# Two key pairs of node tiles to each step of the edge loop, and the twelve steps that this moves everything behind it

## What is computed

```python
xn = layernorm(x)
# 1. graph attention over the edges
Wh = xn @ W_w + W_b
e  = leaky_relu((Wh @ a_w[:256])[dst] + (Wh @ a_w[256:])[src] + a_b[0], 0.2)
att = segment_softmax(e, src)
g  = relu(segment_sum(att[:, None] * Wh[dst], src))
# 2. linear attention over all nodes, 8 heads
q, k = elu(xn @ Wq.T) + 1, elu(xn @ Wk.T) + 1;  v = xn @ Wv.T
m  = (q (k^T v) / max(q . sum(k), 1e-6)) @ Wproj.T + bproj
x  = x + g + m
# 3. mixture of 8 experts, two of them for each node
t  = layernorm(x);  combine = top-2 of softmax(t @ router_w.T), renormalised
out = x + t + sum_e combine[:, e] * (gelu(t @ w1[e] + b1[e]) @ w2[e] + b2[e])
```

## Time and profile before

| | before |
|---|---|
| median of 3 runs | 2332.44 us |
| lowest, highest | 2324.99, 2332.51 us |
| profiled execution, its own time | 2342.57 us |
| its span | 2340.8 us |
| PE, DVE, ACT, POOL busy, share of the span | 76%, 72%, 40%, 42% |
| granted TensorE clock, mean | 0.862 |

### The profile page before, as it was taken

One profiled execution on the slowest core, in us unless ns is written; L12 is line 12 of the kernel. 1 busy time (PEld: TensorE's weight loads), 2 busy tenths in 40 slices (PEclk: granted clock), 3 DMA queues, 4 the chain that ended last, 5 costly groups with the idle time before them and its releaser, 6 DMA issues.

```text
span 2340.8 us, 40197 instructions
## 1 busy us (share of the span) xinstructions
PE 1768.7 (76%) x13588; PEld 1284.2 (55%) x13588; DVE 1674.4 (72%) x4215; ACT 934.8 (40%) x2258; POOL 984.9 (42%) x996
## 2 busy tenths in 40 slices
PE   4788886651666676578888757887788787899998
PEld 2557573441455564466666535555555555666666
DVE  5888898652665667667676668888888878865665
ACT  6222221121222222222222236656656566666564
POOL 3000002425655566655555666666666566100000
PEclk7788797785878887788988869989999999999999
DMA  5011111113545543333333333333333348300000
GB/s 164 6 55 49 48 62 30 45 60 90 140 129 137 137 126 106 93 101 102 100 99 96 83 91 83 85 90 94 81 91 84 91 81 88 35 10 10 10 19 12
DMA packets 121715, 182.20 MB, mean 78 GB/s; under 512 B 21614, under 2 KB 92158, under 8 KB 121470
## 3 DMA queue, kind: packets, MB, share of 16 engines
q0 software_dynamic: 45568, 120.06, 21.8%
q1 hardware_dynamic: 75904, 59.25, 8.1%
HBM read 152.43 MB, written 26.63 MB: 76 GB/s over the span
## 4 chain that ended last, share of the span: by engine, by line
DVE 37%; PE 31%; issue 14%; another core or an unknown queue 9%; ACT 4%; DVEq 2%; POOL 1%; DMA 1%; ACTq 0%; SPq 0%; POOLq 0%
PE bank L1197 6%; PE bank L1213 6%; DVE big L1458 4%; DVE mloc L1541 3%; DVE big L1463 3%; DVE work L1536 3%; DVE work L1519 2%; PE bank L928 2%; DVE big L1460 2%; DVE big L1465 2%; DVE scr L1563 2%; DVE work L1737 2%; PE bank L903 1%; PE bank L1083 1%
## 5 line engine op out<-in xcount | busy, mean ns | idle before, releaser
L631 POOL DMA_INDIRECT work<-table,tiles x904 | 906.8, 1003 | 574.0 <-PE bank L1065 312.4
L1213 PE MATMUL bank<-big 128*128 128x256 f16 x2352 | 314.2, 277 | 0.3 <-issue 0.3
L1063 PE MATMUL bank<-work,scr 128*128 128x257 f16 x904 | 277.7, 307 | 36.5 <-issue 22.1
L1064 PE MATMUL bank<-work,scr 128*128 128x256 f16 x904 | 279.4, 309 | 14.8 <-issue 14.8
L1065 PE MATMUL bank<-work,scr 128*128 128x257 f16 x904 | 279.4, 309 | 12.5 <-issue 12.5
L1197 PE MATMUL bank<-scr,big 128*128 128x512 f16 (+1 forms) x1248 | 280.3, 374 | 4.1 <-ACT big L838 2.9
L1031 PE MATMUL bank<-identh,work 128*128 128x128 f16 x904 | 85.3, 250 | 247.1 <-DVE work L1536 209.7
L1213 PEld LDWEIGHTS bank<-big 128*128 128x128 f16 x2352 | 233.8, 99 | 35.7 <-issue 0.5
L1563 DVE SCALAR_TENSOR_TENSOR scr<-scr,gg,bank 128x257 f32<-128x257 f32 x452 | 217.9, 482 | 38.3 <-issue 15.2
L954 PE MATMUL bank<-big 128*128 128x208 f16 x1568 | 172.6, 264 | 72.9 <-DVE big L1465 62.2
L1031 PEld LDWEIGHTS bank<-identh,work 128*128 128x128 f16 x904 | 64.8, 112 | 278.8 <-DVE work L1536 229.0
(11 more groups left out here) (337 smaller groups left out, 3383.3 us busy)
## 6 DMA issues: line engine op xcount, KB each, us to landing
work<-table,tiles POOLq DMA_INDIRECT x904
scr<-normed_cols SPq DMA_DIRECT2D x98, 128.0 KB
table<-big SPq DMA_DIRECT2D x49, 129.0 KB, 2.2
normed_rows<-scr SPq DMA_DIRECT2D x49, 128.5 KB, 2.8
big<-normed_rows SPq DMA_DIRECT2D x49, 128.5 KB
normed_cols<-big SPq DMA_DIRECT2D x49, 128.0 KB, 2.7
xs<-in_x_dram SPq DMA_DIRECT2D x4, 1536.0 KB, 14.6
out_dram<-work SPq DMA_DIRECT2D x48, 128.0 KB
```

Source lines behind the costliest of these rows:

```text
L631: pool.indirect_dma_start(G[:, r, j, :], None, table, bass.IndirectOffsetOnAxis(ap=col[:, t:t + 1], axis=0)).then_inc(rows_in[r // GS], 16)
L1063: pe.matmul(of[:, 0:D + 1], hi, Gh[:, r, j, 0:D + 1], start=(j == 0), stop=False)
L1064: pe.matmul(of[:, 0:D], hi, Gh[:, r, j, D + 2:2 * D + 2], start=False, stop=False)
L1213: mm = pe.matmul(of, hTp[ph][:, k % 2, f, (j + c) * P:(j + c + 1) * P], w2p[pw][:, e, f, :], start=False, stop=(f == 1 and m == 2))
```

## The change

`K_AT` gives each step from -1 to 11 two pairs of node tiles (the last step one), so that the keys end at step 11 and not 23. `CTX_AT`, `A_AT` and `F_AT` are counted from there and all come 12 steps earlier (13, 18 to 42, 51 on); the last expert step is 12 steps earlier too. The experts' weights are placed behind the keys, in steps 14, 16, ... 28, and `b2` at step 30. The two pairs of a step use two banks (7 and 1), two `kk` and two pairs of `ev` and `rv`; PE does both `keys` of a step first and then both `key_sums`. SP asks for columns one step ahead of the rows. In the node table SP sends the rows of tile i + 2, the columns of i + 1 and the table's row of i - 1 in one round. ACT's `norms` is cut into halves, two tiles at the end of one step and two at the end of the next.

```diff
-        kk = q_[0].rearrange("p a b -> p (a b)").rearrange("p (j c) -> p j c", j=2)
+        kk = [v.rearrange("p a b -> p (a b)").rearrange("p (j c) -> p j c", j=2) for v in q_]
...
+        evs, rvs = (ev, qd), (rv, mm_)
...
-        K_AT = {p - 1: p for p in range(PW)}
+        K_AT = {s: range(2 * s + 2, min(2 * s + 4, PW)) for s in range(-1, -(-PW // 2) - 1)}
         CTX_AT = max(K_AT) + 2
         A_FROM = CTX_AT + 5
         A_AT = {A_FROM + p: p for p in range(PW)}
-        P_AT = {1 + 2 * n: n for n in range(2 * PIECES)}
-        assert max(P_AT) < CTX_AT
+        P_AT = {CTX_AT + 1 + 2 * n: n for n in range(2 * PIECES)}
+        B2_AT = max(P_AT) + 2
+        K_BANK = (7, 1)
...
# SP, the node table
-            for i in range(W):
-                rows, r, q = slice(i * P, (i + 1) * P), i % XR, i % TR
-                sp.wait_ge(n_xn, i + 1)
-                sp.dma_start(normed_rows[rows, :], xn[r]).then_inc(rows_out[r], 16)
-                sp.wait_ge(n_xnT, i + 1)
-                sp.dma_start(normed_cols[rows, :], xnT[r].rearrange("p h n -> p (h n)")).then_inc(cols_out[r], 16)
-                sp.wait_ge(n_fd, i + 1)
-                sp.wait_ge(n_lo, i + 1)
-                sp.dma_start(table[rows, :], tab[q]).then_inc(table_out[q], 16)
+            for i in range(-2, W + 1):
+                if i + 2 < W:
+                    sp.wait_ge(n_xn, i + 3)
+                    sp.dma_start(normed_rows[of_tile(i + 2), :], xn[(i + 2) % XR]).then_inc(rows_out[(i + 2) % XR], 16)
+                if 0 <= i + 1 < W:
+                    sp.wait_ge(n_xnT, i + 2)
+                    sp.dma_start(normed_cols[of_tile(i + 1), :], xnT[(i + 1) % XR].rearrange("p h n -> p (h n)")
+                                 ).then_inc(cols_out[(i + 1) % XR], 16)
+                if i > 0:
+                    sp.wait_ge(n_fd, i)
+                    sp.wait_ge(n_lo, i)
+                    sp.dma_start(table[of_tile(i - 1), :], tab[(i - 1) % TR]).then_inc(table_out[(i - 1) % TR], 16)
...
# SP, the edge loop
             for s in range(-1, NS):
-                if s in K_AT:
-                    p = K_AT[s]
-                    if p > 1:
-                        sp.wait_ge(k_ps, p - 1)
+                if s == -1:
+                    for p in K_AT[s]:
+                        turned_rows(p, p)
+                for p in K_AT.get(s + 1, ()):
+                    sp.wait_ge(k_ps, p - 1)
                     turned_rows(p, p)
+                for p in K_AT.get(s, ()):
                     if p > 1:
                         sp.wait_ge(k_sum, p - 1)
                     for j in range(of_pair[p]):
...
# ACT
             def keys_raw(p):
                 n = of_pair[p] * D
                 act.wait_ge(k_ps, p + 1)
-                if p:
-                    act.wait_ge(k_kk, p)
+                if p > 1:
+                    act.wait_ge(k_kk, p - 1)
...
-                for j in range(of_batch[b]):
+                first, n = halves(b)[h]
+                for j in range(first, first + n):
...
                 if s + 3 in FIRST:
-                    norms(FIRST[s + 3])
+                    norms(FIRST[s + 3], 0)
+                if s + 2 in FIRST and of_batch[FIRST[s + 2]] > 2:
+                    norms(FIRST[s + 2], 1)
...
# PE
-                if s - 1 in K_AT:
-                    key_sums(K_AT[s - 1])
-                if s in K_AT:
-                    keys(K_AT[s])
+                for p in K_AT.get(s, ()):
+                    keys(p)
+                for p in K_AT.get(s - 1, ()):
+                    key_sums(p)
...
# DVE
-                if s - 1 in K_AT:
-                    keys_one(K_AT[s - 1])
+                for p in K_AT.get(s - 1, ()):
+                    keys_one(p)
...
-                if s == CTX_AT + 1:
+                if s == B2_AT + 1:
                     dve.wait_ge(loaded["b2"], 16 * 2)
```

43 lines of the change are left out of this document (23 added, 20 removed).

## The result

The changed kernel takes 2269.28 us (median of four, 2266.97 to 2273.09) beside 2331.55 us of the kernel before: a ratio of 0.9747, 95% interval 0.973 to 0.9765. The forecast was 2303.6 us, the range 2273 to 2333. The sign is right, the gain is 62 us where 29 were forecast, and it lies outside the range. The profiled execution took 2273.09 us with a span of 2271.3.

A forecast was written before the change was run, and what follows sets the result against it. The prediction took the chain through the whole edge loop into the experts' matmuls as the bound, with PE ending each key step. Its parts summed to -28.8 us from the median 2332.44 us: 2303.6 us, range 2273 to 2333.

The forecast's parts named there:

- Part 2: Key steps: twelve get a second pair, 16 more float32 matmul records ahead of the spreading, 4.4 us each: +52.8 us.
- Part 1: Edge loop: twelve key steps go and twelve joint steps (edges and experts together) come: +8.6 us.
- part 4: Tail behind the last edges: it loses twelve expert steps of 5.97 us: -71.6 us.
- part 3: Experts' weights leave the key steps, -18.1 us, and land in two context and six query steps, +12.0 us.
- part 5: Norms cut into halves: -1.5 us in nine batches among edges, -0.5 us in four in the tail: -15.5 us.
- part 6: The split of `b2` goes from a context step to a query step: +3 us, between 0 and 6.
- part 7: Node table: SP's new order frees ACT's 104 us wait, but DVE sets the pace: 0, at most -5 us.
- Part 8: SP's loads of columns and rows, four tiles of each a step, cause no wait: taken as 0.
- the second pair comes cheap: Rival, doubled key steps: clock rises from 0.82 to 0.96, 2287 us, or half the pair finds slack, 2277 us; chance 0.23.
- The rule that the forecast cites: Dense matmuls keep PE at full rate; doubled key steps would run at the joint steps' clock: 2287 us.
- The rival of the late release: Key steps: a second pair repeats ACT's delayed release, costing 7.7 us, not 4.4: 2343 us, or slower; chance 0.09.

The follow-up runs named there:

- one pair per step: The change with one pair of node tiles per step again, 25 key steps, all else kept: 2341.15 us in one group, 2323.41 us in another beside the change.
- the version with the loads ahead: The change, weights still behind the keys, with each load of weights issued one step ahead: 2132.44 us, ratio 0.9864, on a quicker chip.
- second profile of the change: The changed kernel itself, unaltered, run again in a later group: 2269.83 us, ratio 0.9746.
- the change with the norms mixed: The change with norms halved only among edges and whole behind the last edges: 2132.84 us, ratio 0.9855, on a quicker chip.
- with filler: The change with one pair of node tiles per step and 32 unread f16 transposes ahead of the turn in the key steps: 2325.44 us, ratio 0.9981.

## Why the prediction was wrong

Its parts against what the runs show (slower chips, the kernel before at 2330 us):

- **Part 2, the second pair, is the step that failed**: +52.8 us forecast, twelve times 4.4. Measured 0.8 us a step (12.76 against 11.96), some 10 us. The forecast's lower end was 0, and its reason was the right one: "the step with one pair is no longer than the contexts' step without". It was set aside with "the first pair has used up the slack". It had not: PE is idle 3.29 us in a step with one pair and 2.05 in one with two. The 48 us of DVE's waiting for PE was read as the price of any further work there. But that wait grew by far less than the work: (48.0 + 16.0) / 25 = 2.6 us a step before, and in the change 50.7 + 2.9 us in 13 steps, 4.1 us. What the runs show in its place, on one chip: the second pair lengthens PE's part of the step by 2.3 us, not by its full 3.4 to 3.8, since the clock goes from 0.85 to 0.96; and the release of the spreading, which came 1.75 us late with one pair, comes 0.23 us late with two. The forecast had read both as PE's work. In the kernel before, more float32 work costs nearly its full length (1.4 to 1.8 us for eight products); in the changed one it costs 0.7. The order itself is worth 0.2 to 0.9 us of a step. Why the release comes on time in the doubled steps stays open.
- **Part 1 and part 4**: twelve steps moved, +8.6 and -71.6 us. Behind the last reduction the change saves 325.3 - 254.9 = 70.4 us against one pair per step, to 1.2 us as forecast.
- **Parts 3, 5, 6 and 7**, forecast -18.1 + 12.0 - 15.5 + 3 + 0 = -18.6 us. One pair per step against the kernel before is these parts together, with the order and the second bank: -6.8 us in one group, +7.9 in another. The norms are the term that was mis-sized: -15.5 forecast, 0 to -4 measured, since the four batches in the tail lose 4.4 us and weren't given a loss. From the profile of the kernel before to that of one pair per step the key steps lose 22.6 us and the queries' gain 18.2, where part 3 has -18.1 and +12.0; the order and the banks lie in these numbers too. Alone, on a quicker chip, moving the weights cost 6 us.
- **Part 8**, loads: no wait, as forecast. What the forecast didn't see is that SP's new wait delays whatever is behind it. It did no harm only because the weights had been moved: with them back in the key steps the time is 49 us longer.

So the sum was wrong by 43 us at the pair and by 12 to 27 us the other way in the rest, and the two partly cancelled: that the total missed by 34 us and not by more is luck.

Three smaller readings of the forecast don't hold. The 1.8 us for which DVE is held before L1632 (part 3) are 26.3 / 23 = 1.1 us by its row. The ends of parts 3, 5 and 6, added up, lie 20.5 us below and 33.5 us above the forecast, where its own range has 13.6 and 13.4. And the ends of parts 5 and 7 are 5.5 and 5 us off, where the floor of the whole range counts 4 for both.

Of the rivals, "the second pair comes cheap" is what happened, and with more than either of its reasons gives. The clock rose as it said, to 0.95, and PE's other work shrank by about the 1.3 us that it counts; the half that it didn't see is the late release that went away, 1.5 us a step. Its other reason, slack in the step with one pair, was right in kind: the slack was this release. The rule that the forecast cites (the Trainium skill, "TensorE: Matmul & The Clock Gate", "Loop structure matters more than you think") is borne out by the granted clock, 0.95 with two pairs and 0.83 to 0.85 with one; the time worked out by it, 2287 us, is still 18 too long. The rival of the late release, at 7.7 us a pair, had the direction wrong: with a second pair the delay did not double, it went.

## What to carry to other kernels

When work is added to an engine that others wait for, the wait says that the engine matters, not that further work costs its full length. Set the engine's idle time per step and the length of the nearest step without such work beside it, read how long after the engine's last record the waiting one starts, and price the addition in the kernel in which it will stand. Before moving a wait on an in-order queue, list what stands behind it: here a load that nobody had touched would have cost most of what the change gave (48 of 62 us). And work packed into fewer steps can be cheap where the clock is low (0.85 here), since it makes its neighbours quicker.

## What the runs showed of the hardware

**The same kernel at 2331 and at 2162 us.** The kernel before takes 2330 to 2333 us in three groups and 2162 to 2163 in two, with little spread in each. Where the traces of the two kinds can be set side by side, the difference lies in how late PE's results reach the others. On a slower chip, in the change (start us, us, engine, line; two rows far apart on two engines, the last product of the spreading and the scores that wait for it):

```profile
1199.67 0.17 PE L1063 MATMUL bank<-tiles,work 128*128 128x2 f16 x1
...
1204.38 0.17 DVE L1521 TENSOR_TENSOR s<-bank,work 128x8 f32<-128x8 f32 x1 [1.52 <-remote]
```

On a quicker chip, in the version with the loads ahead:

```profile
1069.94 0.16 PE L1063 MATMUL bank<-tiles,work 128*128 128x2 f16 x1
...
1070.14 0.17 DVE L1521 TENSOR_TENSOR s<-bank,work 128x8 f32<-128x8 f32 x1
```

4.5 us between the record's end and the reader in the one (DVE has other work for the first 3 of them and is idle for the last 1.5), 0.04 in the other. Matched to the records that make them, 67 of 418 releases by PE come over 1.5 us late in the 60 joint steps of the second profile of the change, and none of 555 in the same steps of the three changed kernels of the third group. The key steps of the fourth group have 6 such releases in 13 steps with two pairs and 44 in 25 with one. Steps without keys or experts take 12.1 us on a slower chip and 9.9 us on a quicker one, and they differ in one part only: from the scores to `turn` 3.11 and 3.14 us, from there to the end of `spread` 5.72 and 5.60, from there to the next scores 3.29 and 1.23. The stretch behind the last reduction is equal on both (254.9 us in the change and with the loads early), and the sorting and the table, some 40 us shorter on the quicker chips, were not cut in this way. So the "late release" of the forecast is no property of float32 work, as it was taken for there.

It also covers part of the second pair's price. A step with one pair is 261.7 / 25 = 10.5 us on a quicker chip (the kernel before with the weights moved, so in the old order), one with two pairs 161.2 / 13 = 12.4: 1.9 us, where it is 0.8 on a slower one. PE's part grows by as much on both (2.4 and 2.3 us); the time from the end of `spread` to the scores, which the second pair shortens, gives back 0.5 us on the one and 1.5 on the other. And the ratio of the change with the norms mixed is 0.9855 there. Without the norms' 4.4 us that would be about 0.9875, a gain of 27 us, as an estimate; the change itself was not run on such a chip. What delays the releases stays open: nothing in the traces names it, and no run here was made to find it. The granted clock alone it is not: with filler, at 0.92, the release of the spreading was later than without, at 0.85. Open, too, is why the queries' steps are 8.5 us longer with one pair per step (350.4 us) than in the change (341.9), with the same instructions.
